# Input products of a GRU cell for up to four steps at once, kept in a ring in SBUF

## The reference

```python
def cell(h, x):
    gi = x @ W_ih + b_ih
    gh = h @ W_hh + b_hh
    ...
    r = jax.nn.sigmoid(i_r + h_r)
    z = jax.nn.sigmoid(i_z + h_z)
    n = jnp.tanh(i_n + r * h_n)
    h_new = (1.0 - z) * n + z * h
...
def _derivative(q, p, drive, coupling, bias):
    i_couple = jnp.tanh(q) @ coupling.T
    dq = q - q ** 3 / 3.0 - p + drive + i_couple + bias
    dp = EPSILON * (q + ALPHA - BETA * p)
```

## Time and profile before

| | |
|---|---|
| Time, median of 3 runs | 1513.64 us (1509.73 to 1516.41) |
| Profiled execution | 1517.27 us, span 1515.2 us |
| Recurrences | from about 599 us of the span to its end |
| One step in the middle | 14.0 us |
| Busy share of the span | PE 96%, PEld 84%, DVE 84%, ACT 60%, POOL 51% |
| Mean granted TensorE clock | 0.988 |

### The profile page before, as it was taken

How to read it: one execution, slowest core, us unless ns; L and a number is a source line. 1 busy time by engine, 2 the same in 40 slices (tenths; PEclk the granted TensorE clock), 3 DMA queues, 4 the chain that set the end, 5 groups by cost and what they waited for, 6 DMA issues and landing times.

```text
span 1515.2 us, 94439 instructions
## 1 busy us (share of the span) xinstructions
PE 1453.9 (96%) x41966; PEld 1279.7 (84%) x41966; DVE 1275.0 (84%) x3095; ACT 902.3 (60%) x2753; POOL 768.6 (51%) x916
## 2 busy tenths in 40 slices
PE   4799999999999999999999999999999999999997
PEld 2366766666766669999999999999999999999996
DVE  6888888778888776788888889889888888888887
ACT  5567766757767743555555555555555555555553
POOL 2567777757677756443444344344444434434432
PEclk8899999999999999999999999999999999999999
DMA  7477777767777772000000000000000000000000
GB/s 258 82 158 167 162 154 161 166 146 169 170 171 176 153 163 79 12 11 15 15 12 15 15 12 15 15 12 15 16 15 11 15 15 12 15 15 12 15 15 14
DMA packets 188216, 108.74 MB, mean 72 GB/s; under 512 B 134272, under 2 KB 165184, under 8 KB 187808
## 3 DMA queue, kind: packets, MB, share of 16 engines
q1 hardware_dynamic: 187360, 102.45, 28.7%
q10 hardware_dynamic: 448, 0.25, 0.1%
HBM read 50.65 MB, written 11.67 MB: 41 GB/s over the span
## 4 chain that ended last, share of the span: by engine, by line
PE 79%; DVE 9%; DMA 4%; issue 3%; SPq 2%; ACT 1%; POOL 1%; DVEq 0%; ACTq 0%; POOLq 0%
PE psB L1463 35%; PE psA L1492 15%; PE psQ L1174 10%; PE psA L1497 8%; PE psQ L1220 4%; PE psO L1266 3%; DMA first<-qn 2%; DMA PT<-front 2%; PE psO L1254 2%; PE psB L1202 1%; DVE psA L830 1%; SPq L325 1%; DVE qn L770 1%; DVE room L801 1%; DVE oT L893 1%
## 5 line engine op out<-in xcount | busy, mean ns | idle before, releaser
L1463 PE MATMUL psB<-first,Wx 128*128 128x64 f16 x9216 | 290.7, 193 | 1.8 <-issue 1.3
L1492 PE MATMUL psA<-ts,Cp 128*128 128x64 f16 x8160 | 281.0, 193 | 7.1 <-ACT ts L1563 6.4
L1463 PE MATMUL psB<-first,Whh 128*128 128x64 f16 x9072 | 286.2, 193 | 0.8 <-POOL first L1928 0.5
L1174 PE MATMUL psQ<-Wx,front 128*128 128x512 f16 x1152 | 280.1, 391 | 5.5 <-DVE front L982 4.6
L1463 PEld LDWEIGHTS psB<-first,Wx 128*128 128x128 f16 x9216 | 278.0, 98 | 2.8 <-issue 2.4
L1463 PEld LDWEIGHTS psB<-first,Whh 128*128 128x128 f16 x9072 | 273.7, 98 | 1.4 <-POOL first L1928 0.6
L1492 PEld LDWEIGHTS psA<-ts,Cp 128*128 128x128 f16 x8160 | 256.3, 98 | 8.3 <-ACT ts L1563 7.2
L1563 ACT ACTIVATE ts<-qst 128x256 f16<-128x256 f32 x192 | 80.1, 417 | 298.0 <-DVE qst L1676 298.0
L1174 PEld LDWEIGHTS psQ<-Wx,front 128*128 128x128 f16 x1152 | 107.5, 100 | 124.3 <-issue 12.3
L1928 POOL TENSOR_TENSOR en<-rz,dn 128x256 f32<-128x256 f32 x64 | 46.7, 730 | 259.5 <-issue 256.8
L1497 PE MATMUL psA<-ts,Cp 128*128 128x64 f16 x4080 | 161.2, 193 | 0.0
(11 more groups left out here) (199 smaller groups left out, 2899.8 us busy)
## 6 DMA issues: line engine op xcount, KB each, us to landing
rows<-rows_dram SPq DMA_DIRECT2D x64, 256.0 KB, 4.3
front<-in_x SPq DMA_DIRECT2D x32, 256.0 KB, 4.3
XR<-in_x_turned SPq DMA_DIRECT2D x32, 256.0 KB, 4.8
out<-ob SPq DMA_DIRECT2D x63, 128.0 KB, 1.8
x<-x SPq DMA_DIRECT2D x29, 224.0 KB
Whh<-in_W_qkv SPq DMA_DIRECT2D x12, 256.0 KB, 8.3
room<-in_W_hh SPq DMA_DIRECT2D x12, 256.0 KB, 2.7
room<-in_W_ih SPq DMA_DIRECT2D x12, 256.0 KB, 2.9
```

The source lines that it names most:

```text
L1174: last = mm(psQ[:, n, :], xn[p.u][:, i, c, :], Wqkv[:, j, c, n * D:(n + 1) * D], start=(c == 0 and t == 0), stop=(c == KC - 1 and t == 2))
L1463: last = mm(o, W_[:, i, c, g * PART:(g + 1) * PART], src[:, j, c, :], start=False, stop=False, skip_group_check=True)
L1492: mm(psF[:, s % 2, m, :], Cp[:, i, c, m * PART:(m + 1) * PART], ts_[:, 0, c, :], start=(c == 0 and m == 0 and i == 0), stop=False, skip_gr ...
```

## The change

The products of x and W_ih are taken out of the steps. The cells 3 to 62 are put in groups (`CELLS`): sizes 1, 2, 2, then twelve groups of 4, then 2, 2, 1, 1, 1. While the steps of one group run, TensorE computes the next group's x times W_ih, with the columns of all its cells in one matmul: 256 columns for four cells. Each of the 12 output chunks of a group is summed in one of two PSUM banks (`psX`, psQ 0 and 1, by turns), and ScalarE moves it with the bias to a ring of two groups in SBUF (`gx`, by `keep`). A group's 12 chunks are spread evenly over the steps of the group before; half of a step's chunks stand in the first filler, half in the second. `seed_rz` now copies from the ring in place of the bias; for the new gate, `gate_b` adds the ring's part and `seed_n` seeds only the h part.

Beside this, `sq` moves into the bank of `th`, the cell's tanh into the second half of `psN`, and `PA` into SBUF. With that `low_t` waits for `sq_done`, `seed_n` waits for `h_done` and stands behind `high_h`, `square` of stage 2 stands ahead of `high_h`, and `gh_front` waits for the seeds. x is split into a ring `xg`, a group ahead. Cells 0 to 2 and 63 stay as they were. In the attention part, semaphores are merged in pairs with the same order of work (left out below).

```diff
--- before.py
+++ after.py
...
@@ -1417,14 +1417,46 @@
     qs = [sb(f"qst{s}", F) for s in range(3)]
     ws, rs = sb("cub", F), sb("rest", F)
     ob = two("ob", F)
+    LEN = 4
+    CELLS = [[3], [4, 5], [6, 7]] + [list(range(n, n + LEN)) for n in range(8, 56, LEN)] + [[56, 57], [58, 59], [60], [61], [62]]
+    xg = [sb(f"xg{u}", [PART, 2, KC, LEN, B], F16) for u in range(2)]
+    gx = [sb(f"gx{u}", [PART, GC, LEN, B]) for u in range(2)]
+    GROUP = {n: g for g, cells in enumerate(CELLS) for n in cells}
+    STEPS_OF = [[0]] + [list(range(CELLS[g - 1][0] - 2, CELLS[g][0] - 2)) for g in range(1, len(CELLS))]
+    assert sorted(GROUP) == list(range(3, T - 1)) and sum(STEPS_OF, []) == list(range(T - 4))
+
+    def chunks_in(n):
+        for g, steps in enumerate(STEPS_OF):
+            if n in steps:
+                per = GC // len(steps)
+                return g, range(steps.index(n) * per, (steps.index(n) + 1) * per)
+        return None, range(0)
+
+    def turned_in(n):
+        for g, steps in enumerate(STEPS_OF):
+            if n in steps:
+                cells = CELLS[g + 1] if g + 1 < len(CELLS) else [T - 1]
+                return [c for k, c in enumerate(cells) if steps[k * len(steps) // len(cells)] == n]
+        return []
+
+    def place_of(n):
+        g = GROUP[n] if n < T - 1 else len(CELLS)
+        return g, (n - CELLS[g][0] if n < T - 1 else 0)
+
+    def xs_of(n):
+        if n < 3:
+            return xs1 if n == 1 else xs
+        g, k = place_of(n)
+        return xg[g % 2][:, :, :, k, :]
 
     def bank(name, k):
         return banks[name][:, k, :].rearrange("p (v c b) -> p v c b", v=2, c=KC)
 
-    psRZ, psN, psF, psT, psQ, psH, psE = (bank(*k) for k in (("psB", 0), ("psB", 1), ("psA", 0), ("psA", 1), ("psQ", 0), ("psQ", 1), ("psQ", 2)))
+    psRZ, psN, psF, psT, psE = (bank(*k) for k in (("psB", 0), ("psB", 1), ("psA", 0), ("psA", 1), ("psQ", 2)))
+    psX = banks["psQ"]
     psS = banks["psO"][:, :, :].rearrange("p c n -> p (c n)").rearrange("p (v c b) -> p v c b", v=2, c=KC)
-    th, sq = psT[:, 0, :, :], psQ[:, 0, :, :]
-    nn, PA = psH[:, 0, :, :], psH[:, 1, :, :]
+    th, sq = psT[:, 0, :, :], psT[:, 1, :, :]
+    nn, PA = psN[:, 1, :, :], sb("PA", F)[:, :, :]
     E1, E2 = psE[:, 0, :, :], psE[:, 1, :, :]
     SQ, SP = psS[:, 0, :, :], psS[:, 1, :, :]
 
@@ -1474,6 +1506,21 @@
             gate_products(Wih, xs1 if n == 1 else xs, 1, range(GC // 2, 2 * KC))
             pe.wait_ge(S["seeded_n"], n + 1)
             gate_products(Wih, xs1 if n == 1 else xs, 1, range(2 * KC, GC)).then_inc(S["gi_done"], 1)
+
+        def products_of_group(g, parts):
+            N = len(CELLS[g]) * B if parts else 0
+            for m, c in parts:
+                j = g * GC + m
+                if c == 0:
+                    if m == 0:
+                        pe.wait_ge(S["xs_ready"], CELLS[g][-1] + 1)
+                    need(pe, S["gx_kept"], j - 1)
+                for k, (i, jj) in enumerate(TERMS):
+                    last = mm(psX[:, j % 2, 0:N], Wih[:, i, c, m * PART:(m + 1) * PART],
+                              xg[g % 2][:, jj, c, :, :].rearrange("p t b -> p (t b)")[:, 0:N],
+                              start=(c == 0 and k == 0), stop=(c == KC - 1 and k == 2), skip_group_check=True)
+                if c == KC - 1:
+                    last.then_inc(S["gx_done"], 1)
 
         def gh_front(n):
             pe.wait_ge(S["hs_ready"], n + 1)
@@ -1508,12 +1555,20 @@
             gh_back(1)
 
         def step(t):
+            g, ms = chunks_in(t.n)
+            parts = [(m, c) for m in ms for c in range(KC)]
             if t.n:
                 stage(t, 0)
-            gi_front(t.n + 2)
+            if t.n == 0:
+                gi_front(2)
+            products_of_group(g, parts[:len(parts) // 2])
             stage(t, 1)
-            gi_back(t.n + 2)
+            if t.n == 0:
+                gi_back(2)
+            products_of_group(g, parts[len(parts) // 2:])
             stage(t, 2)
+            pe.wait_ge(S["seeded_rz"], t.n + 3)
+            pe.wait_ge(S["seeded_n"], t.n + 3)
             gh_front(t.n + 2)
             stage(t, 3)
             gh_back(t.n + 2)
@@ -1529,13 +1584,13 @@
             stage(t, 0)
             pe.wait_ge(S["xs_ready"], cell + 1)
             pe.wait_ge(S["seeded_rz"], cell + 1)
-            gate_products(Wih, xs, 1, range(0, KC + 1))
+            gate_products(Wih, xs_of(cell), 1, range(0, KC + 1))
             stage(t, 1)
-            gate_products(Wih, xs, 1, range(KC + 1, 2 * KC))
+            gate_products(Wih, xs_of(cell), 1, range(KC + 1, 2 * KC))
             pe.wait_ge(S["seeded_n"], cell + 1)
-            gate_products(Wih, xs, 1, range(2 * KC, 2 * KC + 2))
+            gate_products(Wih, xs_of(cell), 1, range(2 * KC, 2 * KC + 2))
             stage(t, 2)
-            gate_products(Wih, xs, 1, range(2 * KC + 2, GC)).then_inc(S["gi_done"], 1)
+            gate_products(Wih, xs_of(cell), 1, range(2 * KC + 2, GC)).then_inc(S["gi_done"], 1)
             pe.wait_ge(S["hs_ready"], cell + 1)
             gate_products(Whh, hs, 0, range(0, KC - 1))
             stage(t, 3)
@@ -1570,16 +1625,35 @@
                 act.wait_ge(x2_done, B)
                 act.wait_ge(S["gi_done"], 1)
             elif n > 2:
-                act.wait_ge(S["gi_done"], n)
-            a((xs1 if n == 1 else xs)[:, 0, :, :].rearrange("p c b -> p (c b)"), xr(n)).then_inc(S["xs_hi"], 1)
+                need(act, S["gx_done"], (place_of(n)[0] - 1) * GC)
+            a(xs_of(n)[:, 0, :, :], XR[:, :, :, n]).then_inc(S["xs_hi"], 1)
 
         def seed_rz(n):
             need(act, S["sig_done"], n)
-            a(both(psRZ), both(seedRZ)).then_inc(S["seeded_rz"], 1)
+            if n in GROUP:
+                g, k = place_of(n)
+                act.wait_ge(S["gx_kept"], (g + 1) * GC)
+                a(psRZ.rearrange("p v c b -> p (v c) b"), gx[g % 2][:, 0:2 * KC, k, :]).then_inc(S["seeded_rz"], 1)
+            else:
+                a(both(psRZ), both(seedRZ)).then_inc(S["seeded_rz"], 1)
 
         def seed_n(n):
-            need(act, S["bn_done"], n)
-            a(both(psN), both(seedN)).then_inc(S["seeded_n"], 1)
+            need(act, S["h_done"], n)
+            if n in GROUP:
+                a(flat(psN[:, 0, :, :]), flat(seedN[:, 0, :, :])).then_inc(S["seeded_n"], 1)
+            else:
+                a(both(psN), both(seedN)).then_inc(S["seeded_n"], 1)
+
+        def keep(g, ms):
+            N = len(CELLS[g]) * B if ms else 0
+            for m in ms:
+                j = g * GC + m
+                act.wait_ge(S["gx_done"], j + 1)
+                if m == 0 and g > 1:
+                    act.wait_ge(S["bn_done"], CELLS[g - 2][-1] + 1)
+                    act.wait_ge(S["seeded_rz"], CELLS[g - 2][-1] + 1)
+                bias = seedRZ[:, m // KC, m % KC, 0:1] if m < 2 * KC else seedN[:, 1, m - 2 * KC, 0:1]
+                a(gx[g % 2][:, m, :, :].rearrange("p t b -> p (t b)")[:, 0:N], psX[:, j % 2, 0:N], ACT.Identity, bias=bias).then_inc(S["gx_kept"], 1)
 
         def sigmoids(n):
             act.wait_ge(S["rz_done"], n + 1)
@@ -1615,6 +1689,7 @@
             q, k = state(t, s)
             a(ts_[:, 0, :, :], q[:, :, :], ACT.Tanh, scale=k).then_inc(S["ts_hi"], 1)
             need(act, S["ts_ready"], t.n * 4 + s)
+            need(act, S["w_done"], t.n * 4 + s)
             a(th, q[:, :, :], ACT.Tanh, scale=k).then_inc(S["th_done"], 1)
 
         def square(t, s):
@@ -1625,16 +1700,20 @@
         def first():
             high_xs(0)
             high_xs(1)
+            act.wait_ge(S["ts_ready"], 1)
             square(Pair(0, 0, 0), 0)
             sigmoids(0)
             seed_rz(1)
             tanh_n(0)
+            high_h(0)
             seed_n(1)
-            high_h(0)
             high_xs(2)
+            high_xs(3)
             of_p(0)
 
         def step(t):
+            g, ms = chunks_in(t.n)
+            half = len(ms) // 2
             if has(t, 2):
                 sigmoids(t.n + 1)
             if t.n:
@@ -1651,14 +1730,15 @@
                 tanh_n(t.n + 1)
             elif has(t, 1):
                 tanh_n(t.n + 1)
-            if has(t, 2):
-                seed_n(t.n + 2)
+            keep(g, ms[:half])
             tanhs(t, 2)
+            square(t, 2)
             if has(t, 2):
                 high_h(t.n + 1)
-            square(t, 2)
-            if has(t, 3):
-                high_xs(t.n + 3)
+                seed_n(t.n + 2)
+            keep(g, ms[half:])
+            for n in turned_in(t.n):
+                high_xs(n)
             tanhs(t, 3)
             square(t, 3)
             if has(t, 1):
@@ -1680,12 +1760,18 @@
             dve.wait_ge(S["gn_done"], n + 1)
             if n == 0:
                 dve.wait_ge(S["gi_done"], 1)
-            v.tensor_tensor(an[:, :, :], psN[:, 0, :, :], rz[:, 0, :, :], ALU.mult).then_inc(S["an_done"], 1)
+            to = psN[:, 0, :, :] if n in GROUP else an[:, :, :]
```

(46 more changed lines are left out.)

## The result

The changed kernel takes 1576.11 us, the median of 4 runs (1571.17 to 1580.74), against 1514.83 us; the ratio is 1.041 with a 95% interval of 1.0375 to 1.0445. The forecast was 1576. The profiled execution has a span of 1579.0 us, 63.8 more than before.

What follows compares the result with a forecast made beforehand. TensorE bounded the old kernel; the VectorE and ScalarE ring would bind the new. Ring, psX waits, start and end sum to +62.5 us: 1580 on the profiled 1517.3, forecast 1576 from the median, range 1545 to 1592.

Steps and rivals of the forecast that it cites:

- The price of a product: TensorE's input products: 256 columns take 109.1 ns where four of 64 take 116.7, so a step 13.73 us, not 14.0.
- The ring of VectorE and ScalarE: Loop `add_f`, tanh, `low_t`, `cubic`, `rest`, `add_f`: the square's wait adds 0.77 us, making 14.32 a step, +0.32.
- The ring's own 13.55: Length of the VectorE and ScalarE loop freed from TensorE, read in step 61: 13.55 us, 0.45 below TensorE's 14.0.
- the 10.44 us: Part of the loop's length in step 61, from q2 (1472.96) to the last `add_f` (1483.40).
- The waits for the psX banks: Chunk j waits for the `keep` of chunk j-2, lengthening steps with six or twelve chunks; without these waits 23 us less.
- The end groups: Last short groups: steps 58 and 59 at 18.2 us (+4.25 each) from two banks and `keep` latency, step 60 +0.3.
- the clock only as a rival: Waits of step 1 or 58 halve the granted clock, or the ring takes 0.5 a step: 1585 to 1610, chance 0.04.
- Start and end: Step 0 +7.3 us from cell 3's products, seed and psX waits; end +3.2 from steps 61 to 63.
- The two seed stalls: TensorE waits for `seed_n(1)`, 1.3 us, of which about 0.5 passes on, and for `seed_n(2)` in step 0, about 1.75.
- The work ahead: Group g is multiplied during group g-1's steps: step 1 does 8.0 us of group products, steps 4 and 5 7.9 each.
- The light steps: Steps 50 to 53 have only 2.0 us of group products, step 60 none; TensorE's saving there is lost.

Runs made afterwards that it cites:

- run 3: The kernel before with one line changed, `low_t` waiting for the square (`sq_done`) in place of `th_done`: 1541.55 us, 1.0175.
- run 6: The changed kernel with the square in SBUF in stages 1 and 3 alone, `low_t` waiting for `th` there: 1553.86 us, 1.0259.
- run 4: The changed kernel with half a step's chunks sharing one bank in groups of one or two cells, step 1 as before: 1551.82 us, 1.024.
- run 1: The changed kernel with the square in its own SBUF tile and `low_t` waiting for `th` again: 1559.05 us, 1.0285.
- run 7: The changed kernel with run 4 and run 6 together, and the cell's tanh in SBUF so `seed_n` stands behind `tanh_n` again: 1525.99 us, 1.0073.
- run 8: The kernel of run 7 with groups of two cells (128 columns) in place of four: 1517.26 us, 1.0021.
- run 2: The changed kernel with the square in its own SBUF tile, `low_t` still waiting for the square: 1626.61 us, 1.073.

## Why the prediction was right

- **The price of a product.** 109.1 ns for 256 columns (109.0 from the two ends as printed), measured 108.9. The products are cheaper as forecast, and steps that the ring sets don't let it out.
- **The ring of VectorE and ScalarE.** 14.32 us, measured 14.32. Shown from two sides: the wait alone slows the kernel before to 14.51 (run 3), and without it in stages 1 and 3 the changed kernel falls to 13.92 (run 6, where 13.86 was expected). The ring's own 13.55 was read at the end of the trace, where TensorE had room. Two readings on the way were off without touching the sum. VectorE also waits 0.23 us a step for GpSimd, ahead of the new h, which the prediction's list of its waits leaves out; that wait lies within the 10.44 us and so within the 13.55. And `low_t` of stage 0 was to wait 0.7 us and waits 0.53: in the middle of the kernel before, a sigmoid stands ahead of stage 0's tanh on ScalarE, and the tanh starts 0.66 us after the clip (1019.82). In the changed kernel it starts 0.46 us after it (1023.10), as at the end of the trace. ScalarE's rows, before and after:

```profile
1020.48 0.41 ACT L1563 ACTIVATE ts<-Qs 128x256 f16<-128x256 f32 x1
```

```profile
1023.56 0.42 ACT L1618 ACTIVATE ts<-Qs 128x256 f16<-128x256 f32 x1
```

- **The waits for the psX banks.** Of the 23 us forecast, 20 lay in the steps that run 4 packs. It gave 1576.11 - 1551.82 = 24.3, and about 4.3 of them are what steps 58 and 59 took beyond their forecast at the slower clock, below.
- **The end groups.** Here the term was mis-sized. Steps 58 to 60 were given 18.2, 18.2 and 14.3 us and took 19.52, 21.23 and 15.33, 5.4 more in all. The waits for `keep` stand where they were forecast: the third chunk starts 2.13 and 2.12 us after q2 in steps 58 and 59, where 2.23 or later was given. But behind some of them the granted clock fell to 0.50, the lower of its two levels (1.2 GHz), and products and stages took up to 1.90 us in place of 1.10. In step 60 it is not `keep`: with no input products at all, TensorE waits 1.14 and 2.13 us for the ring, and the clock falls behind the second wait (run 4 shows the same). The prediction named the clock only as a rival, with a chance of 0.04, and argued from waits of 0.9 us in which it had held. It passed over a row of the same trace. In stage 0 of step 63 of the kernel before, TensorE waits 2.42 us, and its next 32 products take 1.80 us at a granted clock of 0.55:

```profile
1499.12 1.80 PE L1492 MATMUL psA<-ts,Cp 128*128 128x64 f16 x32 [2.42 <-ACT ts L1563]
```

```profile
1499.10:1500.70 1.60, 1.58 (x32) 1.58 (x33) 1.23 (x4) 0.88 (x3) 0.40 (x1) 0.55 0.00 0
```

  The length of the wait alone doesn't decide it. Whole steps (columns as in the earlier trace rows, the clock third from the end), in this order: step 57 of the changed kernel (waits of 1.63 and 1.76 us), step 59 of run 1 (1.53 and 1.76), step 60 of run 7 (1.13 and 2.08) and of run 8 (1.14 and 2.08):

```profile
1461.41:1477.31 15.90, 12.51 (x424) 12.27 (x421) 12.75 (x35) 8.73 (x26) 5.19 (x7) 1.00 0.04 11
```

```profile
1482.25:1500.35 18.10, 14.58 (x477) 13.99 (x472) 12.98 (x36) 11.18 (x33) 6.30 (x8) 1.00 0.04 11
```

```profile
1466.76:1480.68 13.92, 10.69 (x349) 10.36 (x350) 12.47 (x36) 7.30 (x20) 5.28 (x7) 1.00 0.04 12
```

```profile
1457.43:1472.46 15.03, 11.97 (x349) 11.70 (x350) 12.47 (x35) 7.30 (x20) 5.29 (x7) 0.89 0.04 13
```

  Where the clock held, in run 1, step 59 took 18.10 us, near the 18.2 forecast (a middle step of run 1 is 0.25 us shorter). So the waits were priced about right, and what the term left out is the clock.
- **What makes up for that.** Against a flat 14.0 us a step, steps 0 to 60 take 64.3 us more, and the end 3.4: 5 over the forecast, nearly all of it the clock. But the kernel before took 3.6 us more than a flat 14.0 over the same steps (a step now and then takes 0.3 to 0.8 more), which the sum left out; the changed kernel's middle steps hold 0.8 of that kind. So the profiled span grew by 63.8 where the sum gave 62.5. That the median meets the forecast within 1 us is luck: these two misses stand against each other, and the four runs lie 9.6 us apart.
- **Start and end.** +7.3 and +3.2 us forecast, +7.2 and +3.4 measured. The 7.3 holds 0.5 for the stall ahead of step 0's q2, which the 7.2 leaves out; from the first product of the recurrences to q2 of step 1 it is 7.7. The two seed stalls of 1.3 and 1.75 us are rows of 1.25 and 1.74, and run 7, which takes them away with the psX waits of step 0, saves 3.1 there.
- **The work ahead.** Even with most of the new waits gone (run 7) the kernel isn't faster: steps 0, 1, 4 and 5 hold about 4 + 6.4 + 8.0 us of extra products and waits, and a middle step gives back 0.08. The light steps give nothing, as their ring is no shorter.

## What to carry to other kernels

When an engine is full and you shorten its work, look up the ring of dependent operations that hides under it, at a place in the trace where that engine has room; here it was 0.45 us shorter than the step, and one wait of up to 0.31 us, felt in three of four stages, used it up. Here a bank was freed by putting two tiles in one, and the reader of the one then waited for the writing of the other; price such a wait in the ring before the saving. Work done ahead must be paid at the start, and is given back at the end only if nothing else sets the pace there.

## What the runs showed of the hardware that was not expected

- A VectorE operation with both inputs in SBUF stood behind GpSimd: 0.97 us in place of 0.42, ending 0.28 us after GpSimd's operation (run 2); where it came first, GpSimd's operation took 0.85 us in place of 0.73. A tile moved from PSUM to SBUF to avoid a wait of 0.77 us a step brought one of 0.54 in its place (run 1).
- The granted clock fell to 0.50 behind waits of 1.89 us (step 58), 1.63 and 1.72 (step 59) and 2.13 (step 60) of the changed kernel, and stayed at 1.00 behind 1.63 and 1.76 in step 57; step 60 kept it in run 7 and not in run 8, with the same waits. What decides it stays open.
